# Reordering the setup, the attention steps and the weight splits of a fused adaLN, conv-attention and mixture-of-experts kernel

## The reference, cut to what matters

```python
mod = (silu(c) @ wmod).reshape(B, 6, 1, D)          # sa, ca, ga, sb, cb, gb
h = layernorm(x) * (1 + ca) + sa
x = x + ga * attn(h)
h = layernorm(x) * (1 + cb) + sb
x = x + gb * ffn(h)

def attn(x):                                        # DI = 256
    h = linear(rmsnorm(x) * norm_w, in_w, in_b)
    gate, val = sigmoid(h[..., :DI]), h[..., DI:]
    a = (dwconv(val, 4 taps) @ A) @ Bm
    b = linear(silu(dwconv(val, 9 taps)), pw)
    y = gate * linear(concat(linear(a, ha), linear(b, hb)), fuse)
    return x + linear(y, out_w)

def ffn(x):                                         # 160 experts, 8 taken, inner size 64
    probs = sigmoid(x @ router + bias)
    w = top8(probs); w = 2.5 * w / (sum(w) + 1e-9)
    routed = sum over all e of (silu(x @ w_gate[e]) * w[e]) @ w_down[e]
    return routed + silu(x @ shared_up) @ shared_down
```

## Time and profile before

| | us |
|---|---|
| median of 3 executions (lowest to highest) | 540.15 (539.52 to 541.37) |
| the profiled execution | 539.89 |
| its span in the trace | 537.6 |
| TensorE busy in the span | 519.5 |
| VectorE busy | 483.1 |
| ScalarE busy | 419.5 |
| POOL busy | 33.4 |

### The profile page before, as it was taken

How to read it: one execution, slowest core, us unless ns; L and a number is a source line. 1 busy time by engine, 2 the same in 40 slices (tenths; PEclk the granted TensorE clock), 3 DMA queues, 4 the chain that set the end, 5 groups by cost and what they waited for, 6 DMA issues and landing times.

```text
span 537.6 us, 7260 instructions
## 1 busy us (share of the span) xinstructions
PE 519.5 (97%) x2474; PEld 246.2 (46%) x2474; DVE 483.1 (90%) x609; ACT 419.5 (78%) x685; POOL 33.4 (6%) x57
## 2 busy tenths in 40 slices
PE   7888999989999999999999999999999999999996
PEld 5344444434444444544444444544444444444442
DVE  6877999999999997999889997899989989999995
ACT  6558997989797867798597876688899777777774
POOL 6110200410000000120000000020000000000000
PEclk9899999999999999999999999999999999999999
DMA  8895654545544764546535755446645756656650
GB/s 275 302 383 231 230 186 157 187 143 182 156 158 147 253 201 132 180 158 198 180 121 170 226 188 186 158 156 202 200 169 195 231 194 222 199 196 200 205 183 20
DMA packets 33595, 102.92 MB, mean 191 GB/s; under 512 B 3732, under 2 KB 8984, under 8 KB 33560
## 3 DMA queue, kind: packets, MB, share of 16 engines
q1 hardware_dynamic: 33560, 102.47, 57.2%
HBM read 99.57 MB, written 2.36 MB: 190 GB/s over the span
## 4 chain that ended last, share of the span: by engine, by line
PE 76%; DVE 12%; ACT 7%; issue 5%; POOL 1%; ACTq 0%; DVEq 0%; POOLq 0%
PE bank L1137 24%; PE bank L1138 23%; PE bank L1139 23%; DVE g_all L1104 2%; DVE s_all L1108 2%; ACT s_all L797 1%; ACT g_all L816 1%; PE bank L1276 1%; PE bank L1286 1%; DVE attw L1022 1%; DVE w L947 1%; PE bank L1132 1%; PE bank L1360 1%; ACT L797 1%; ACT L774 1%
## 5 line engine op out<-in xcount | busy, mean ns | idle before, releaser
L797 ACT ACTIVATE s_all<-bank 128x512 f32<-128x512 f32 x320 | 189.5, 595 | 83.8 <-PE bank L1139 80.3
L1104 DVE TENSOR_TENSOR g_all<-s_all,g_all 128x1024 f16<-128x1024 f32 x160 | 195.6, 1223 | 35.7 <-ACT g_all L816 35.2
L1108 DVE TENSOR_TENSOR s_all<-s_all,c_all 128x1024 f32<-128x1024 f32 x160 | 195.2, 1220 | 0.0
L816 ACT ACTIVATE g_all<-s_all 128x1024 f16<-128x1024 f32 x160 | 168.4, 1052 | 2.7 <-DVE s_all L1108 2.6
L1137 PE MATMUL bank<-g_all,w 128*128 128x512 f16 x320 | 121.3, 379 | 2.9 <-DVE g_all L1104 2.9
L1137 PE MATMUL bank<-x_h,w 128*128 128x512 f16 x320 | 121.4, 379 | 2.4 <-ACT s_all L797 2.2
L1138 PE MATMUL bank<-g_all,w 128*128 128x512 f16 x320 | 121.3, 379 | 0.0
L1139 PE MATMUL bank<-g_all,w 128*128 128x512 f16 x320 | 121.3, 379 | 0.0
L1139 PE MATMUL bank<-x_l,w 128*128 128x512 f16 x320 | 121.3, 379 | 0.0
L1138 PE MATMUL bank<-x_h,w 128*128 128x512 f16 x320 | 121.3, 379 | 0.0
L1137 PEld LDWEIGHTS bank<-g_all,w 128*128 128x128 f16 x320 | 31.3, 98 | 43.5 <-DVE g_all L1104 7.2
(11 more groups left out here) (221 smaller groups left out, 373.3 us busy)
## 6 DMA issues: line engine op xcount, KB each, us to landing
c_all<-combine SPq DMA_DIRECT2D x160, 512.0 KB, 3.9
w<-w_dram SPq DMA_DIRECT2D x20, 512.0 KB, 10.6
combine<-cT SPq DMA_DIRECT2D x4, 256.0 KB, 3.6
out_dram<-res SPq DMA_DIRECT2D x3, 256.0 KB, 2.5
s_all<-mats_dram SPq DMA_DIRECT2D x1, 640.0 KB, 5.7
attw<-symT_dram SPq DMA_DIRECT2D x1, 576.0 KB, 6.7
c_all<-symT_dram SPq DMA_DIRECT2D x1, 576.0 KB, 7.6
mod<-rows_mod SPq DMA_DIRECT2D x1, 576.0 KB, 4.4
```

The source lines that it names most:

```text
L797: a(sr[J % SRING][:, q * L:(q + 1) * L], U[q][:], ACT.Silu, scale=1.0 / ES).then_inc(s["s_done"], 1)
L816: a(gh[n % GRING], sr[n % SRING], ACT.Copy).then_inc(s["hi_set"], 1)
L1104: e.tensor_tensor(gl[n % GRING], sr[n % SRING], gh[n % GRING], ALU.subtract).then_inc(s["lo_set"], 1)
L1108: e.tensor_tensor(sr[J % SRING], sr[J % SRING], cr[J % CRING], ALU.mult).then_inc(s["gm"], 1)
```

## The change

No operation is added or removed; one wait is added. The calls of `walk` and of the table stand in a new order. The table before and after, cut to the steps that are spoken of below (`...` marks what is left out), and the setup list's end:

```diff
 WITH = (
     {
-        0: ((6, "split_hi"),),
-        1: ((2, "nb"), (7, "split_hi"), (7, "split_lo"), (1, "gate"),),
-        3: ((1, "wo"),),
-        4: ((1, "base0"), (8, "split_hi"), (8, "split_lo"),),
-        5: ((1, "ya0"), (1, "tanh0"), (1, "base1"),),
...
-        21: ((1, "turn2"), (2, "tap0"),),
-        22: ((1, "xh"), (2, "tap1"), (2, "conv0:0:1"), (15, "split_hi"), (15, "split_lo"),),
-        24: ((1, "xl"), (16, "split_hi"), (16, "split_lo"),),
-        26: ((1, "logit"), (1, "shup"), (2, "tap4"), (2, "conv0:3:5"), (2, "tap5"), (17, "split_hi"),),
-        27: ((1, "prob"), (17, "split_lo"), (2, "tap6"),),
...
-        33: ((1, "norm"), (2, "tap7"), (2, "conv0:7:8"),),
-        34: ((1, "cT"), (2, "tap8"), (2, "conv0:8:9"),),
-        35: ((1, "cT_sb"), (1, "c_out"),),
+        0: ((1, "conv1:5:9"), (6, "split_hi"), (2, "t1a"),),
+        1: ((1, "gate"), (1, "silu1"),),
+        2: ((1, "ya0"), (1, "ya1"),),
+        5: ((7, "split_hi"),),
+        7: ((7, "split_lo"), (2, "t1b"), (2, "hm"),),
+        8: ((8, "split_hi"), (2, "ha"),),
...
+        23: ((2, "rms"), (1, "o0"), (13, "split_lo"), (2, "hi"),),
+        24: ((2, "low"), (14, "split_hi"), (15, "split_hi"), (1, "o1"), (1, "x2"),),
+        25: ((14, "split_lo"),),
+        26: ((2, "turn"), (1, "bn"), (2, "hnT"),),
+        27: ((1, "rstd2"), (2, "conv0:0:1"), (16, "split_hi"), (1, "nb2"),),
+        28: ((2, "base0"), (1, "t2a"), (15, "split_lo"), (2, "val"), (1, "t2b"),),
+        29: ((2, "conv0:1:2"), (2, "tap0"), (1, "turn2"), (3, "t1a"), (1, "xh"), (1, "xl"), (2, "conv0:2:5"),),
+        30: ((16, "split_lo"), (2, "wo"), (1, "logit"), (1, "prob"), (1, "max"), (1, "swap"), (2, "conv0:5:6"),),
+        31: ((2, "conv0:6:7"), (1, "cw"),),
...
+        35: ((2, "base1"), (1, "ss"), (2, "tap1"), (1, "cT"), (1, "cT_sb"),),
+        36: ((2, "tap2"), (1, "c_out"),),
+        37: ((19, "split_hi"), (19, "split_lo"), (3, "t1b"), (2, "conv0:8:9"), (2, "z"),),
+        38: ((2, "zh"),),
     },
     {
-        0: ((2, "z"),),
-        3: ((2, "zmv"), (2, "wo"),),
-        4: ((2, "gate"), (2, "base0"),),
-        5: ((2, "ya0"), (2, "tanh0"), (2, "base1"),),
...
-        26: ((2, "logit"), (2, "shup"), (3, "tap4"), (3, "conv0:3:4"),),
-        27: ((2, "prob"), (3, "tap5"), (3, "conv0:4:5"), (3, "tap6"), (3, "conv0:5:6"),),
+        0: ((2, "zl"),),
+        3: ((2, "tap3"),),
+        4: ((2, "tap4"),),
+        7: ((2, "gate"), (2, "tap5"),),
+        9: ((2, "tap6"), (2, "silu0"),),
+        13: ((2, "tap7"),),
+        15: ((2, "zmv"),),
+        17: ((2, "tap8"),),
...
+        26: ((3, "low"), (2, "ya1"), (2, "yb1"), (2, "gy0"), (2, "gy1"),),
+        27: ((2, "o0"), (2, "o1"), (2, "x2"), (2, "bn"), (2, "rstd2"),),
+        30: ((2, "t2a"),),
+        31: ((3, "conv0:0:1"), (2, "t2b"), (3, "conv0:1:2"), (2, "turn2"), (2, "xh"), (2, "xl"), (3, "val"),),
+        32: ((2, "logit"), (2, "prob"), (2, "max"), (2, "swap"), (2, "cw"), (2, "shup"), (2, "sum"), (3, "tap0"),),
+        37: ((3, "z"), (3, "tap1"),),
+        38: ((3, "tap2"), (3, "zh"), (3, "tap3"), (3, "conv0:5:6"), (3, "tap4"),),
     },
     {
-        27: ((3, "logit"), (3, "shup"), (3, "prob"), (3, "max"),),
-        28: ((3, "ss"),),
+        29: ((3, "logit"), (3, "prob"), (3, "shup"), (3, "max"), (3, "swap"),),
+        39: ((3, "ss"),),
     },
```

The wait, in VectorE's `setup(6)`:

```diff
                     shift_gain(rows, s["row_set"])
+                    dve.wait_ge(s["mod_set"], 5)
                     gate_gain(rows, gmag[0:B], gsgn[0:B], s["row_set"])
```

More of the change, by code:

```diff
@@ new lines @@
+    {
+        2: ((3, "tap5"),),
+        4: ((3, "base1"), (3, "zl"),),
+        5: ((3, "tap6"),),
+        7: ((3, "tap7"), (3, "zmv"), (3, "tap8"), (3, "gate"), (3, "conv0:6:7"),),
+        8: ((3, "tanh0"),),
+        9: ((3, "conv0:7:9"), (3, "tanh1"), (3, "silu0"), (3, "silu1"),),
+        13: ((3, "ya0"), (3, "ya1"), (3, "yb0"), (3, "yb1"),),
+        14: ((3, "gy0"), (3, "gy1"),),
+        17: ((3, "o0"), (3, "o1"), (3, "x2"), (3, "bn"), (3, "rstd2"),),
+        19: ((3, "nb2"),),
+        23: ((3, "t2a"), (3, "t2b"),),
+        24: ((3, "turn2"),),
+        27: ((3, "xh"), (3, "xl"),),
+        29: ((3, "logit"), (3, "prob"), (3, "shup"), (3, "max"), (3, "swap"),),
+        32: ((3, "cw"), (3, "sum"),),
@@ L210, in walk @@
     att(0, "val")
+    att(0, "tap0")
     att(0, "z")
-    setup(15)
-    att(0, "tap0")
-    setup(20)
-    att(0, "zh")
-    setup(13)
-    att(0, "zl")
-    att(0, "zmv")
-    setup(22)
-    att(0, "conv0:0:9")
-    att(1, "stat")
-    setup(8)
-    att(0, "tap1")
-    att(0, "base0")
-    att(0, "tap2")
-    att(0, "gate")
-    setup(3)
+    att(1, "stat")
+    att(0, "tap1")
+    att(0, "zh")
+    att(0, "base0")
+    att(0, "table")
+    att(0, "tap2")
+    att(0, "tap3")
+    setup(13)
@@ L228, in walk @@
+    att(0, "conv0:0:9")
+    att(0, "zl")
+    setup(20)
     att(1, "nb")
[L229 removed]
     att(0, "tap4")
     att(0, "tap5")
+    split_hi(0)
+    setup(15)
+    att(1, "t1a")
+    setup(3)
+    att(1, "t1b")
     att(0, "tap6")
     att(0, "tap7")
[L234 to L235 removed]
+    att(0, "silu0")
+    att(0, "zmv")
+    att(0, "gate")
+    setup(7)
     att(0, "tap8")
[L237 to L242 removed]
@@ L275, in walk @@
-    att(0, "t2a")
-    att(0, "t2b")
-    split_hi(1)
-    att(0, "turn2")
-    att(1, "conv0:6:9")
-    att(0, "xh")
-    split_lo(1)
-    att(0, "xl")
-    att(0, "logit")
-    att(0, "shup")
-    att(0, "prob")
-    att(0, "ss")
-    att(1, "silu0")
-    att(1, "conv1:0:5")
+    split_lo(1)
+    att(1, "wo")
+    att(0, "nb2")
+    setup(8)
+    split_hi(2)
+    att(1, "z")
+    setup(11)
+    att(1, "zh")
+    split_lo(2)
+    att(0, "t2a")
+    att(1, "conv0:0:6")
+    att(1, "zl")
+    att(0, "t2b")
@@ L289, in walk @@
+    split_hi(3)
+    att(0, "turn2")
+    att(0, "xh")
+    att(0, "xl")
+    att(1, "conv0:6:9")
+    att(0, "logit")
+    att(0, "prob")
+    split_lo(3)
+    att(1, "zmv")
     att(0, "max")
     att(0, "swap")
+    split_hi(4)
     att(0, "cw")
+    split_hi(5)
     att(0, "sum")
-    split_hi(2)
-    split_hi(3)
+    att(0, "shup")
+    att(1, "conv1:0:5")
+    att(0, "ss")
+    att(2, "stat")
+    att(1, "silu0")
     att(0, "cT")
+    att(1, "base0")
+    split_lo(4)
+    split_lo(5)
     att(0, "cT_sb")
-    att(1, "conv1:5:9")
+    att(2, "nb")
```

166 lines of the change are left out of this document (49 added, 117 removed), and 3 rows, old and new, of the table WITH.

## The result

| | before | after |
|---|---|---|
| median, us (lowest to highest) | 540.76 (539.52 to 541.55), 4 runs | 534.23 (533.65 to 534.51), 4 runs |
| profiled execution / its span | 539.89 / 537.6 | 534.51 / 532.2 |

The ratio is 0.988, 95% interval 0.9857 to 0.9903: 1.2% faster. I forecast 0.33% with a range down to 535.5, so the sign was right and the size outside the range.

What follows compares the result with a forecast made beforehand. VectorE was taken to bound item 0's expert stream and TensorE those of items 1 and 2. The sum was 539.89 - 2.1 + 0.3 = 538.1 us, given as 538.3 for the median, range 535.5 to 541.5.

Steps and rivals of the forecast that it cites:

- Step 1: Setup's VectorE chain, reordered with a later row load: taken as 0, bounds -1 and +1.5 us.
- Step 2: ScalarE's table in the setup: a sigmoid load on the chain from logit to cT of item 0, +1.0 us.
- rival C: Setup loses nothing (-1) and the 1.3 us of chains don't appear: 536.0 us; chance 0.12.
- Step 3: Work done ahead of item 0's stream: TensorE 0.8 to 1.0 us behind, VectorE's first product 1.3 us later.
- Step 4: Item 0's stream: VectorE's work net -4.1 us, 1.3 us of chain waits; TensorE -2.1 us in work done.
- new chain waits: Waits from item 1's second half drawn into few slots of item 0's stream: 1.3 us, between nothing and 3.3.
- Step 5: Items 1 and 2's streams: TensorE's work the same, possible waits +0.3 us, bounds 0 and 2 x 3.3 us.
- A: Item 0's stream: the late second half takes VectorE's 4.1 us back as waits, first product later: 540.2 us; chance 0.20.
- B: TensorE waits at logit and up once an item, slots 29 to 34, 3.3 us each: 543.1 at 5 us; chance 0.18.

Runs made afterwards that it cites:

- e5: The changed kernel with the dummy sigmoid (table load) moved back behind nb2 of item 0: 535.67 us, ratio 0.9899.
- x5: The kernel before with base0, base1, x2 of item 1 and hm, ha, low, six taps of item 2 cut to 8 columns: 539.22 us.
- x1: The kernel before with tap3 to tap8 of item 2 cut to 8 columns, in the same slots: 540.48 us, ratio 0.9998.
- e6: The changed kernel with item 2's second half spread over slots 20 to 36 of item 1's stream: 539.40 us, ratio 0.9984.
- e11: The kernel before with only the 13 weight splits of item 0's stream moved to their new slots: 547.66 us, ratio 1.0134.
- e12: The kernel before with the 13 splits in their new slots and tap3 to tap8 of item 2 cut to 8 columns: 548.21 us, ratio 1.0138.
- e10: The changed kernel with item 0's slots in the old order, six taps still moved out, 13 splits in their new slots: 547.06 us, ratio 1.0106.
- e4: The kernel after with the setup list of before, new table kept, item 2's t1a in slot 4: 539.75 us, ratio 0.9981.
- e4b: The kernel after with the setup list of before, new table kept, item 2's t1a in slot 6: 537.86 us, ratio 0.9944.
- x2: The kernel before with tap3 to tap8 of item 3 cut to 8 columns, in the same slots: 540.55 us, ratio 0.9994.
- x3: The kernel before with base0 and base1 of item 1 cut to 8 of 128 channels: 540.25 us, ratio 0.9984.

## Why the prediction was right and wrong

- **Step 1 (setup chain, 0): about right, and its shape too.** The late row load, the 1.2 us wait of `hm` and the cover held; the setup came out 0.6 to 1 us earlier, inside my bound of -1.
- **Step 2 (table load on the chain, +1.0): failed.** I priced the load behind the logits of item 0. The trace shows it ahead of them (46.64 against 48.38), and e5 shows that moving it gains nothing. cT at 53.50, not later than 54.1, was the prediction's own sign for rival C. The 1.38 us of drain that the Trainium skill ("ScalarE: Activation LUTs", section "What ACT_TABLE_LOAD costs") adds to a load doesn't show in this trace: the load at 147.93 stands behind its logits, and its activation starts 1.29 us after it.
- **Step 3 (+0.8 for TensorE, +1.3 for VectorE): failed as a consequence**, with -0.6 and -0.64 measured. What was left of it is the wait of the second product for its combine weights, 1.13 us, which held up no matmul by more than 0.3 us.
- **Step 4 (-2.1): the failed step that carries the miss.** It put item 1's stream 2.1 us earlier in equal work, and by the table of the result it was 4.8 (0.6 and 4.2). Two things in the step were wrong.
  - It took VectorE's product of duo 40 as the end of the stage, which it isn't. Before, TensorE no longer waited from 167 us on while VectorE went on without a gap until 184.6: it was working off backlog inside its two-slot lead. The end belongs to TensorE's waits, and those I had too small. I took the 3.8 us of idle time in the busy union for the ceiling of the stage, and expected 2.3 of them to go. By the union 2.7 went (115.18 to 117.85), but by starts the waits were 5.8, of which 4.1 went, and the way of the stream is 4.2 us shorter, more than the ceiling. This is 1.5 of the missing 2.7 us.
  - It had the product itself near 183.1, and it came at 181.87, the other 1.2 us: it began 1.9 us earlier than I had it (steps 2 and 3), and VectorE idled 2.2 us of 119 in the stream, against 0.3 of 123 before, where I had put 1.3. That 181.87 is so near the 181.8 of the count without chain waits is luck: two errors cancel.

  VectorE's load, on which the step's -4.1 rests, explains only the backlog group (x5: 1.9 us), and the six taps, which are that -4.1 net, bring nothing by themselves (x1). The start and the router chain, 3.5 us before and 1.6 after, went with the order. The 1.3 us of new chain waits turned out as 1.05 at the logits and 0.3 later, in place of the old chain's 2.2.
- **Step 5 (+0.3): -0.6 measured.** The two streams are 121.4 and 118.6 us long, not 124 and 116 as before, since more of item 3's work has moved to the later one. The 0.6 us of waits in item 1's stream went; e6 shows the risk was real for another placing. Waits for `c_out` and for the added semaphore didn't appear.
- **The rivals.** A and B fell: no stretch has the waits that they need. C had the right signs (setup -1, no net chain waits) but was built on the same -4.1 of VectorE and ended at 536.0, 1.8 above the median.

Left open: whether drawing the second half together is itself worth anything beyond the 0.8 us of router chain in item 0's stream and the 0.6 in item 1's, which of the attention steps that left slots 12 to 19 removes the backlog, and what in the first slots of the new table removes the waits of the start.

## What to carry to other kernels

Where two engines are nearly level, list the waiting instructions of the one that sets the end, by start times, and price a change by which of these waits it reaches; the sum of work that it takes off the other engine is only an upper bound for one kind of them. Count a wait from start to start against the pace of the same kind of instruction elsewhere: the busy union showed 3.8 us of 5.8 here. I would place the steps of a short dependent chain with table loads where the engine that sets the end has queued work across it, though no run here isolates that. Try a new order as a whole: its halves gave 0.4% and 0.6% of 1.2%, and single reversals lost half to three quarters of it.

## What the runs showed of the hardware

**A table load can run ahead of the wait of its activation, or behind it.** In the kernel after, that of item 0's `prob` starts at 46.64, before the logits are there at 48.38, and its 1.28 us are free, since ScalarE would idle anyway. Those of items 1 to 3 start only with the logits (147.93, 275.03, 388.44) and cost 1.29 us on the chain. Which of the two it is has to be read from the trace.

**A long wait of TensorE costs twice.** Behind waits of 3.5 us (e11, e12) and 4.6 us (e10) for a weight piece the granted clock fell to half for eight or nine matmuls, 1.6 to 1.7 us more. Behind the shorter waits of item 0's streams, the longest 1.9 us, it stayed at 1.00.

**POOL starves beside VectorE.** One addition of 128x4 numbers, `mse` of item 2, took 12.33 us in the kernel after, 4.29 before and 1.35 in x5. POOL and VectorE of the kernel after:

```profile
85.84 12.33 POOL L588 TENSOR_TENSOR mse<-ms,eps 128x4 f32<-128x4 f32 x1 [27.05 <-ACT hr_h L683]
98.26 1.01 POOL L590 TENSOR_TENSOR rms<-mse,mhalf 128x4 f32<-128x4 f32 x1
...
96.90 1.22 DVE L1082 TENSOR_TENSOR s_all<-s_all,c_all 128x1024 f32<-128x1024 f32 x1
98.03 0.68 DVE L1019 SCALAR_TENSOR_TENSOR attw<-attw,bank 128x512 f32<-128x512 f32 x1
```

It ends with the first VectorE instruction that reads a bank; until then eleven wide ones stood back to back, all with both inputs in on-chip memory outside the banks. Before it ended at 102.31, where x2 at 102.16 reads a bank, and in x5 where VectorE paused. The Trainium skill ("SBUF — State Buffer", section "Who interferes with whom") says that a VectorE instruction with two inputs in that memory contends with a POOL instruction that reads it. The trace agrees, and it shows that POOL didn't get in between the eleven instructions either. No matmul waited for it here, because nothing due soon hung on `mse`.

**The start is not repeatable to 1 us**: nine executions of the same setup list had their first duo between 57.21 and 59.45 us. It goes with the granted clock in the setup. From 18 to 22 us the clock was 1.00 in e11 (57.21) and e4 (57.67), 0.91 in the kernel before (57.81), 0.80 in e4b (58.37), 0.77 in x2 (58.22), 0.65 in x3 (58.62) and 0.50 in x1 and x5 (59.42, 59.45); only e12 (1.00, 58.61) stands outside this order. The kernel after had 1.00 there, so a part of the 0.6 us by which its profile starts earlier may be the clock and not the order: of the executions with 1.00, the old list has 57.2 and 57.7, the new one 56.9 and 57.2.
